# One decoder layer, eight elements on one core: the next element's self-attention scores and maxima at the end of a step, its shifted scores and weighting beside the cross attention of the step after

## The reference

```python
x = x + attn(layernorm(x))      # Q, K, V = X @ W.T; rope on Q, K
    # scores = Qr Kr^T / 4, causal mask, softmax, @ V, @ W_o.T
x = x + xattn(layernorm(x), ctx, mask)
    # Q = X @ W_Q; K, V = ctx @ W_K, W_V; mask, softmax, @ V, @ W_O
x = x + ffn(layernorm(x))
    # h = gelu(x @ Wq_fc.T + b + 2 * (x @ A.T) @ B.T), then the same form with W_proj
```

## Time and profile before

| | |
|---|---|
| runs | 650.0, 641.71, 650.45 us; median 650.0 |
| profiled execution, its own time | 650.37 us |
| its span, first to last instruction | 648.6 us |
| mean granted TensorE clock | 0.908 |
| start of the first full step (a=2) | 177.7 us |
| start of the drain | 580.5 us |

### The profile page before, as it was taken

The page is one execution under the profiler, slowest core; times in us unless marked ns, Lnnn a source line. Parts: engine busy times, 40 slices in busy tenths (PEclk is TensorE's granted clock), DMA queues, the critical chain, the costliest instruction groups (busy, mean ns, idle before and its releaser), DMA issues.

```text
span 648.6 us, 11972 instructions
## 1 busy us (share of the span) xinstructions
PE 545.3 (84%) x4526; PEld 457.5 (71%) x4526; DVE 393.7 (61%) x1121; ACT 295.1 (45%) x450; POOL 196.8 (30%) x284
## 2 busy tenths in 40 slices
PE   3768975887998899979997998889898889888846
PEld 3766565765986598759875897769775867577736
DVE  5664437886688448853796279636872678254432
ACT  3423522446634473446444744365435533553314
POOL 4516331416442324232422323141414102411110
PEclk9878777897999799988999799879997999898858
DMA  8483647033130423052112402060205100100000
GB/s 268 169 232 126 212 164 133 2 101 87 33 115 1 92 51 102 15 81 60 64 53 52 88 28 87 3 139 17 83 2 116 42 17 2 43 2 17 1 0 17
DMA packets 47161, 47.28 MB, mean 73 GB/s; under 512 B 14672, under 2 KB 42976, under 8 KB 47104
## 3 DMA queue, kind: packets, MB, share of 16 engines
q1 hardware_dynamic: 45600, 41.57, 24.4%
q0 software_dynamic: 1504, 4.95, 2.1%
HBM read 30.71 MB, written 15.53 MB: 71 GB/s over the span
## 4 chain that ended last, share of the span: by engine, by line
PE 60%; DVE 11%; issue 9%; POOL 7%; ACT 6%; DMA 3%; SPq 3%; ACTq 0%; POOLq 0%; DVEq 0%
PE banks L626 10%; PE banks L628 9%; PE banks L627 9%; PE banks L924 5%; PE banks L868 5%; PE banks L879 4%; PE banks L782 3%; DVE banks L1607 3%; PE banks L768 2%; PE banks L745 2%; POOL work L509 2%; DMA k_stack<-rot_dram 2%; ACT probs L1238 2%; PE banks L821 1%; PE banks L908 1%
## 5 line engine op out<-in xcount | busy, mean ns | idle before, releaser
L1607 DVE CUSTOM_DVE_ANT_0 banks<-banks,causal_qk 128x256 f32<-128x256 f32 (+1 forms) x256 | 84.4, 385 | 15.0 <-PE banks L745 15.0
L509 POOL TENSOR_TENSOR work<-work,rc 128x616 f32<-128x616 f32 x32 | 38.9, 1216 | 152.7 <-DVE rc L1696 152.7
L520 POOL TENSOR_SCALAR_AFFINE_SELECT probs<-probs 128x256 f32<-128x256 f32 x128 | 52.8, 445 | 77.5 <-ACT probs L1238 77.4
L1238 ACT ACTIVATE probs<-banks 128x768 f32<-128x768 f32 x64 | 50.0, 810 | 44.8 <-PE banks L768 34.6
L1205 ACT ACTIVATE work<-banks 77x1024 f32<-77x1024 f32 x32 | 32.7, 1020 | 72.3 <-PE banks L868 72.3
L626 PE MATMUL banks<-k_hi,q_hi 128*128 128x256 f32 (+1 forms) x160 | 54.7, 342 | 2.1 <-DVE q_lo L1480 2.1
L868 PE MATMUL banks<-ident,work 128*77 128x128 f32 x256 | 35.8, 285 | 15.6 <-DVE c_lo L1563 9.6
L627 PE MATMUL banks<-k_lo,q_hi 128*128 128x256 f32 (+1 forms) x160 | 47.5, 297 | 0.0
L1563 DVE TENSOR_TENSOR q_lo<-work,q_hi 128x512 fp32r<-128x512 f32 x32 | 22.3, 696 | 41.0 <-ACT q_hi L1205 41.0
L628 PE MATMUL banks<-k_hi,q_lo 128*128 128x256 f32 (+1 forms) x160 | 47.1, 294 | 0.0
L626 PE MATMUL banks<-wo_hi,c_hi 128*128 128x256 f32 x128 | 40.2, 314 | 7.7 <-DVE c_lo L1563 7.7
(11 more groups left out here) (180 smaller groups left out, 1734.8 us busy)
## 6 DMA issues: line engine op xcount, KB each, us to landing
rot_dram<-rot_s_hi SPq DMA_DIRECT2D x16, 256.0 KB, 2.1
rot_dram<-rot_s_lo SPq DMA_DIRECT2D x16, 256.0 KB, 2.1
q_stack<-rot_dram SPq DMA_DIRECT2D x32, 128.0 KB, 3.2
k_stack<-rot_dram SPq DMA_DIRECT2D x32, 128.0 KB, 3.4
k_raw<-k_dram SPq DMA_DIRECT2D x16, 154.0 KB, 3.3
v<-v_dram SPq DMA_DIRECT2D x8, 308.0 KB
x_in<-in_x SPq DMA_DIRECT2D x8, 256.0 KB, 3.2
q_stack<-rot_dram SPq DMA_DIRECT2D x32, 64.0 KB, 3.3
```

The costliest lines, as they stand in the source:

```text
L509: pool.tensor_tensor(sc2[g % 2], sc2[g % 2], rc2[:, g % 2].rearrange("p g a -> p g a ()").broadcast_to([P, 4, 2, S2]), ALU.mult).then_inc( ...
L520: last = pool.affine_select(out=diagonal, in_=diagonal, compare_op=ALU.is_ge, fill=0.0, base=0, pattern=[[0, 2], [1, P]], channel_multipli ...
L1238: act.activation(probs[:, n:n + 2, :], bank[:, bk:bk + 2, P:4 * P], ACT.Exp, scale=SCALE).then_inc(p_ok, 1)
L1607: last = dve.tensor_tensor_reduce(out=held[:, at], in0=held[:, at], in1=bias, scale=-1.0, scalar=HUGE, op0=ALU.add, op1=ALU.min, accum_out ...
```

## The change

The functions' arithmetic stays. The order lists of all five engines are written anew, in `first()` and in `step`. The scores and maxima in a step are now those of n, beside b's feed-forward part; the shifted scores, exponentials and weighting of a lie among the groups of b's cross attention. `project_v(n)` moves ahead of `scores(n, 0)`. In SP's queue the stacks of n come before the loads of keys and values. `first()` ends with the scores and maxima of element 2. In the opening the weight loads and splits are in another order too. `shifted_bank` is gone: the shifted scores use banks 0 and 1 alone, `transpose_b(b, 0)` uses bank 3, and several waits on semaphores are new because the banks change hands in another order.

Banks, and the new waits on PE:

```diff
-        def shifted_bank(a, g):
-
-            if a == 0 or g < 3:
-                return 0, 1
-            return (5, 2) if g % 2 else (0, 2)
...
-                if not (isinstance(a, int) and a < 2):
-                    pe.wait_ge(att_ok, a - 1)
+                if a == 2:
+                    pe.wait_ge(att_ok, 1)
+                elif a > 2:
+                    pe.wait_ge(s_max, H * a)
+                    pe.wait_ge(mT_ok, 2 * a - 1)
...
                     pe.wait_ge(trig, 2 * rotated)
-                    if not (isinstance(a, int) and a == 0):
-                        pe.wait_ge(xbT_lo, 2 * a - 1)
+                    if a == 1:
+                        pe.wait_ge(x1_ok, 1)
+                    else:
+                        pe.wait_ge(att_lo, a)
...
-                bk, back = shifted_bank(a, g)
-                if g >= back and (a == 0 or g != 3):
-                    pe.wait_ge(p_ok, HH * a + g + 1 - back)
+                    pe.wait_ge(trig, 2 * min(a + 2, NB))
+                    pe.wait_ge(x1_ok, a)
+                else:
+                    pe.wait_ge(p_ok, HH * a + g)
...
+                elif a < NB - 1:
+                    pe.wait_ge(s_max, H * (a + 2))
```

These are `shifted_bank`, `transpose_a`, `scores`, `shifted` and `output_a`. SP in `step`:

```diff
-                if A:
-                    shifts(a, 0)
-                    shifts(a, 1)
+                if N:
+                    stacks(n, 0)
+                    stacks(n, 1)
+                if A:
                     context(a)
                     context_values(a)
                 if N:
-                    stacks(n, 0)
-                    stacks(n, 1)
+                    shifts(n, 0)
+                    shifts(n, 1)
```

PE in `step`, two stretches of it:

```diff
+                queries(b, 2)
                 scores2(b, 0)
                 if A:
-                    scores(a, 0, rotated)
-                queries(b, 2)
-                if A:
-                    scores(a, 1, rotated)
+                    shifted(a, 0)
                 queries(b, 3)
-                if A:
-                    scores(a, 2, rotated)
                 scores2(b, 1)
+                if A:
+                    shifted(a, 1)
                 transpose2(b, 0)
                 if A:
-                    scores(a, 3, rotated)
+                    shifted(a, 2)
+                    weigh(a, 0)
                 weigh2(b, 0)
...
                 output2(b, 3)
                 if A:
-                    shifted(a, 1)
-                    shifted(a, 2)
-                    shifted(a, 3)
-                    shifted(a, 4)
+                    turn_back_a(a)
+                if N:
+                    project_v(n)
+                    scores(n, 0, n + 1)
                 transpose_b(b, 1)
-                if A:
-                    shifted(a, 5)
-                    weigh(a, 0)
+                if N:
+                    scores(n, 1, n + 1)
+                    scores(n, 2, n + 1)
                 narrow(b)
```

The other functions of the second half follow in turn: `scores(n, 3)`, `hidden(b, 0)`, `scores(n, 4)`, `transpose_max(n, 0)`, `hidden(b, 1)`, and so on to `scores(n, 7)`, `project_down(b, 0)`, `output_a(a)`, `transpose_max(n, 1)`, `transpose_a(m)` and the last three `project_down`. ACT in `first()`, where `values2` copies the cross attention's values out of PSUM:

```diff
                 exponentials(0, 7, 2)
+                values2(4)
                 unnormalised(0, 1, 2)
                 attention_hi(0)
-                values2(4)
```

More of the change, by code:

```diff
@@ L1093, in step @@
                 if A:
-                    scores(a, 6, rotated)
-                output2(b, 1)
+                    shifted(a, 6)
                 weigh2(b, 2)
                 if A:
-                    scores(a, 7, rotated)
+                    weigh(a, 2)
+                    shifted(a, 7)
                 transpose2(b, 3)
                 output2(b, 2)
+                if A:
+                    weigh(a, 3)
                 weigh2(b, 3)
                 if A:
-                    transpose_max(a, 1)
-                    shifted(a, 0)
+                    turn_a(a)
@@ L1125, in step @@
                 hidden(b, 2)
[L1126 to L1133 removed]
+                if N:
+                    scores(n, 6, n + 1)
+                hidden(b, 3)
+                if N:
+                    scores(n, 7, n + 1)
+                project_down(b, 0)
                 if A:
@@ L1136, in step @@
                 if N:
-                    project_v(n)
+                    transpose_max(n, 1)
+                if M:
+                    transpose_a(m)
                 project_down(b, 1)
@@ new lines, in step @@
+                xbT_part(b, 1)
+                if N:
+                    maxima(n, 2)
+                    maxima(n, 3)
+                    maxima(n, 4)
+                    maxima(n, 5)
+                narrow_lo(b)
+                if N:
+                    maxima(n, 6)
+                    maxima(n, 7)
+                    split_max(n, 0)
+                    maxima(n, 8)
+                    maxima(n, 9)
+                hidden_lo(b, 0)
+                if N:
+                    maxima(n, 10)
+                    maxima(n, 11)
@@ L1903, in step @@
+                hidden_lo(b, 1)
+                if N:
+                    maxima(n, 12)
+                    maxima(n, 13)
+                    maxima(n, 14)
+                    maxima(n, 15)
+                    split_max(n, 1)
                 hidden_lo(b, 2)
```

460 lines of the change are left out of this document (234 added, 226 removed).

## The result

| | before | after |
|---|---|---|
| median of the runs, us | 649.83 (641.71 to 650.45) | 661.04 (658.99 to 664.0) |
| ratio to before, 95% interval | | 1.0219 [1.0175, 1.0263] |
| profiled execution, own time, us | 650.37 | 658.99 |
| its span, us | 648.6 | 657.2 |
| start of step a=2, us | 177.7 | 188.7 |

The kernel became slower, by 11.2 us between the medians and by 2.2% in the ratio, where 639 us (624 to 656) was forecast. The span grew by 8.6 us: the opening by 10.9; the five steps gave back 1.0 us instead of 11.5, the last step nothing instead of 2.2, the drain 1.3.

What follows compares the result with a forecast made beforehand. No engine was taken as full, so the time is set stage by stage. Five steps -11.5, opening +2, last step -2.2 and drain 0 sum to -11.7 us on 650.4: forecast 639 us, range 624 to 656.

Steps and rivals of the forecast that it cites:

- The first half: Cross attention of b, up to the last `output2`: 40.5 us, between 38.1 and 43, +1.0 us a step.
- A: Rival: first half near its PE floor, 38.9 us, second 24.1, 627 us in all; chance 0.2.
- D: Rival: first-half groups queue behind exponentials and selects, 46 us, from an interval of 7 us on; 666 us; chance 0.12.
- Rival B: The gain cancels: first half 42.1 us, second 25.6, nothing in five steps, 650 us in all; chance 0.2.
- The second half: Feed-forward part of b, set by DVE's chain with the maxima before `output_a`: 24.9 us, from 23.5 to 27, -3.3 a step.
- 0.4: Second half: us added for PE products at the half clock level, the rest taken as hidden under DVE's chain.
- rival C: Clock stays at 1.2 GHz through `hidden` into `project_down`: 7 us, about 4 hidden, +3 a step, 654 us; chance 0.1.
- The opening: 0 to 177.7 us before: +2 us together, from -3 to +9, with -1 for reordered weight loads at the start.
- the wait for `k_stack`: Opening, before the second element's scores: 4.5 of 5.4 us taken back, as SP is free earlier.
- +7.5: End of the opening: 10.3 us of element 2's maxima before `output_a(1)`, less about 3 of feed-forward products now beside them.
- The last step: Step a=7, without a next element: second half -2.7 us, first half +0.5, together -2.2.
- What would show it: Signs named for the changed profile, among them second half 24 to 26 us and first half 39.5 to 42.

Runs made afterwards that it cites:

- e10: The changed kernel with 11 extra products per step, results unread, only in the gap behind `scores(n, 1)`: 647.14 us, ratio 1.0003 to the kernel before.
- e11: The changed kernel with 11 extra unread products per step in a dense place, in front of `scores(n, 7)`, none in the gap: 662.24 us, ratio 1.0228.
- e6: The changed kernel with extra unread products in steps, opening, last step and drain, and the `project_down` weight split earlier: 635.3 us, ratio 0.9797.
- e9: The kernel before with the changed kernel's order up to `transpose_b(0, 0)` and extra unread products in steps, opening and drain: 633.86 us, ratio 0.9802.
- e5: The kernel before with extra unread products in the thin stretch of its own steps: 639.68 us, ratio 0.9873.
- e8: The kernel before with the changed kernel's order up to `transpose_b(0, 0)` on all engines: 639.06 us, ratio 0.9841.
- e3: The changed kernel with 24 extra unread products per step in the gaps at the start of the second half: 646.65 us, ratio 1.0.
- e4: The changed kernel with the `project_down` weight split earlier in the opening, ahead of the copy `unnormalised(1, 1)`: 661.83 us, ratio 1.024.
- e1: The changed kernel with POOL's `residual_bias(b)` moved ahead of the late norm's factor: 661.77 us, ratio 1.0229.

## Why the prediction was wrong

**The first half** (40.5 us, +1.0) was right: 40.7. DVE fell to 24.7 us there, PE stood at 38.1, the groups followed at 5.4 to 6.9 us (one past the 6.5 named as a sign of trouble, without harm). Rivals A and D are out: waits of 2.6 us remained over the floor, no more. Rival B's sum, nothing in five steps, lies near what came (-1.0), but neither of its halves does (42.1 and 25.6 us).

**The second half** (24.9 us) is where it failed for the steps: 26.9 on average. The step that failed reads: "What PE loses at the half level is mostly under DVE's chain: only narrow and the first `hidden`, some 14 products at 0.09 us more, lie on the path that frees `hidden_lo`; I add 0.4." The overlap was wrong: nothing of PE's loss lies under DVE's chain. From `hidden(b, 0)` on PE has no wait up to the next step, and the maxima need PE too, since each quad of `scores` stands behind a `hidden` in a strict queue; so what PE loses to the level goes into the step and delays DVE's chain as well. (The 14 products of the sentence alone would be 1.3 us; how they became 0.4 isn't worked out.) With the gap filled the chain took 17.8 us to `output_a`, where 17.7 was worked out, and the half 24.4. So the chain, `output_a` and the tail were sized rightly, and the 0.4 should have been about 2.4. That DVE's chain alone was counted, and PE's sum never, did no harm there: with the level held the two end within 0.1 us of each other at `output_a`. Five steps: -11.5 forecast, -1.0 measured, -13.0 with the level held (325.7 against 338.7).

That is rival C, given 0.1 and priced at +3 us a step; measured are 2.4 (68.1 less 65.1 is 3.0 in the later steps, where the low level lasts 10.2 us instead of 6.8). Its mechanism was right, its working less so: the level came back in `hidden`, not in `project_down`, so fewer products were slowed, but DVE's chain hid none of them, where C had it hide 4 of 7 us. That its price comes near is partly luck. The argument against it, "from the first `hidden` on PE is dense again", was true and beside the point, since the price is paid in the first two `hidden`. The section on HAM oscillation in the Trainium skill, TensorE: Matmul & The Clock Gate, spoke for C. e10 and e11 bear it out for waits in the same place of each step: the low level is there in each step and gone when the wait is filled. The waits of the page's own example are for DMAs and longer than the 1.53 us here.

**The opening** (+2) was the larger error: +10.9. Its start (-1) and the wait for `k_stack` (-4.5, that wait now 3.03 us) came to -7.2 together, 1.7 more than forecast, within the spread of these parts; but the start gave 4.7 and the part with the wait 2.5, so that the sum is near is luck. The term that failed is "+7.5" for the maxima of element 2: 18.2. With the level held in both orders (42.2 us in e6, which also has the earlier split, 31.1 in e9) the new order costs 11.1 us there. Some 3.6 us of the excess of 10.7 are thus the order itself, and some 7 the level, 0.6 to 0.8 of them the split's. (The 30.5 us of the profile before are also a short one: the same code took 33.3 in e5 and e8, at a clock of 0.78 instead of 0.89.) The 3 us taken off for the products that ran behind `output_a` were right: 3.4 (9.54 less 6.18). What was too small is the 10.3 for the maxima. In e6 they begin 2.6 us behind `turn_back_a`, behind attn_lo and a `hidden_lo` in DVE's queue, and last 11.9 us with the copies and waits between them; and the part ahead of `turn_back_a`, for which the sum had nothing, took 21.4 us against 19.4 in e9, 1.5 of it `project_v`, which now stands there.

**The last step** (-2.2): nothing. Its second half fell from 25.0 to 22.3 us, the 2.7 of the forecast. Its first half rose by 2.6 us where 0.5 was forecast: PE waits there 2.25 us in front of the first `queries` product (1.46 before), and then ran at 1.2 GHz for 6.8 us, where before it ran on at 2.4 GHz. With fillers in both halves (e6) the step was 4.4 us shorter. **The drain** (0): -1.3.

**What would show it.** DVE over 80% busy, `output_a` released by the last maximum, scores waiting for attn_lo: right. The k_stack wait "gone": wrong, 3.03 us are left. The lowest clock "at the start of the second half": it begins there, but reaches through the second `hidden`.

Is the changed order better at all? With the level held in both, its five steps take 325.7 us (e10) against 330.1 (e5), 0.9 us a step; the end of its opening takes 42.2 us against 31.1 in e9. With the last step, 59.6 us in e6 against 64.5 in e9, the two nearly cancel: e6 and e9, both filled throughout, stand at 0.9797 and 0.9802 of the kernel before and can't be told apart. Its gain that lasts is in the start: moved to the kernel before, it alone gives 10 us (e8), and about 5 on top of the fillers (e9 against e5, each against the kernel before on its own chip).

## What to carry to other kernels

- When a change puts short, spaced PE work ahead of dense work, add the half level to the sum for the products behind it, and count it as hidden under another engine's chain only where PE's timeline has waits to hide it in. Here PE had none from `hidden(b, 0)` on, and the chain that was to hide the loss waited for small PE results behind the slowed products.
- A gap in a periodic loop can be tested cheaply: put products into a free PSUM bank inside the wait. If the granted clock goes up and the time down, the level was the price. Here 11 products a step were worth 14 us, and the same ones elsewhere nothing.
- A deeper pipeline pays its longer opening once and gains per step; count both before choosing it for few elements, and compare a stretch of the opening only with executions at the same clock. And look at the parts of a reordering apart: here the start alone was a gain that the rest hid.

## What was not expected of the hardware

- Eleven more products in a stretch (the second half has 116 of this size, 128x256) made it shorter by 2.8 us; the mean granted clock there went from 0.81 to 1.00.
- The level's falls in the opening are not the same in each execution: the same code took between 44.3 us (e6, a mean clock of 0.96) and 49.3 us (e3, 0.78) from `transpose_b(0, 0)` to the first `shifted` of element 1. What decides this was not settled.
- Beside POOL work DVE's two-input copy took 2.27 us (the change) instead of 0.68 (e4), and its norm 1.46 (e1) instead of 0.74 (the change).
